# Projecting the first two context tiles side by side, with VectorE taking the first tile's high part

## The reference

```python
def rms_norm(x, w, eps=1e-6):
    return x * rsqrt(mean(x * x, axis=-1)) * w              # per head of 128

xn = layernorm(x)                                            # 256 x 512, own rows
q, k, v = xn @ wq, xn @ wk, xn @ wv                          # 16, 4 and 4 heads of 128
k_ctx, v_ctx = ctx @ wk_ctx, ctx @ wv_ctx                    # ctx 4096 x 512, 4 heads each
q, k, k_ctx = rms_norm(q, q_norm_w), rms_norm(k, k_norm_w), rms_norm(k_ctx, k_norm_w)
q, k = rope(q), rope(k)                                      # own rows only
out = softmax(q @ concat(k_ctx, k).T * scale + mask) @ concat(v_ctx, v)
x = x + out @ wo
```

## Time and profile before

| | us |
|---|---|
| median of three runs | 1070.31 |
| profiled execution | 1069.87 |
| its span | 1067.9 |
| PE busy | 1044.2 |
| DVE busy | 751.1 |
| ACT busy | 551.4 |
| POOL busy | 139.7 |
| mean granted TensorE clock | 0.997 |

### The profile page before, as it was taken

The page is one execution under the profiler, slowest core; times in us unless marked ns, Lnnn a source line. Parts: engine busy times, 40 slices in busy tenths (PEclk is TensorE's granted clock), DMA queues, the critical chain, the costliest instruction groups (busy, mean ns, idle before and its releaser), DMA issues.

```text
span 1067.9 us, 15861 instructions
## 1 busy us (share of the span) xinstructions
PE 1044.2 (98%) x6109; PEld 904.5 (85%) x6109; DVE 751.1 (70%) x1634; ACT 551.4 (52%) x956; POOL 139.7 (13%) x142
## 2 busy tenths in 40 slices
PE   7999999999999999999999999999998799999998
PEld 5888888877888888888888888888776599999997
DVE  5856777649677777777777777777178676776675
ACT  4444443334766556666655666667035354445442
POOL 4644434330000000000000000004121000000000
PEclk9999999999999999999999999999999899999999
DMA  6758676497004220044102340024520195555540
GB/s 231 250 188 290 200 235 197 153 312 274 1 1 169 79 89 2 1 168 129 40 1 90 118 133 1 1 90 160 223 92 1 62 353 191 187 195 180 187 167 21
DMA packets 64155, 145.77 MB, mean 137 GB/s; under 512 B 3889, under 2 KB 42705, under 8 KB 62673
## 3 DMA queue, kind: packets, MB, share of 16 engines
q1 hardware_dynamic: 64080, 144.77, 39.1%
HBM read 108.55 MB, written 36.21 MB: 136 GB/s over the span
## 4 chain that ended last, share of the span: by engine, by line
PE 92%; DVE 5%; ACT 2%; issue 1%; DMA 0%; POOL 0%; POOLq 0%; ACTq 0%
PE bank L435 41%; PE bank L454 16%; PE bank L556 12%; PE bank L533 11%; PE bank L557 6%; PE bank L596 2%; PE bank L464 1%; DVE conv_acc L1033 1%; PE bank L722 1%; PE bank L609 1%; PE bank L489 0%; DVE conv_acc L1030 0%; DMA w_ctx_raw<-in_w_ctx 0%; ACT xc L1397 0%; PE bank L640 0%
## 5 line engine op out<-in xcount | busy, mean ns | idle before, releaser
L969 DVE TENSOR_TENSOR pT<-bank,pT 128x512 fp32r<-128x512 f32 x272 | 184.7, 689 | 112.7 <-ACT pT L1364 112.4
L1364 ACT CAST pT<-bank 128x512 fp32r<-128x512 f32 x272 | 156.2, 593 | 144.3 <-PE bank L533 140.8
L556 PE MATMUL bank<-pT,vN 128*128 128x512 f32 (+1 forms) x544 | 208.7, 408 | 0.0
L435 PE MATMUL bank<-kT,qT_hi 128*128 128x512 f32 (+2 forms) x576 | 188.6, 408 | 2.1 <-DVE scores L913 2.1
L913 DVE TENSOR_SCALAR_CACHE_REDUCE scores<-bank 128x512 f32<-128x512 f32 x256 | 169.3, 682 | 0.1
L533 PE MATMUL bank<-ident,scores 128*128 128x128 f32 x1072 | 161.3, 272 | 0.4 <-DVE pT L969 0.3
L435 PE MATMUL bank<-fT_hi,e_hl 128*128 128x256 f32 x816 | 156.4, 284 | 2.4 <-DVE fT_lo L1142 1.5
L1335 ACT ACTIVATE scores<-scores,neg_max 128x1024 f32<-128x1024 f32 (+2 forms) x128 | 154.0, 1203 | 5.7 <-DVE neg_max L925 5.7
L557 PE MATMUL bank<-pT,vN 128*128 128x256 f32 (+1 forms) x544 | 152.1, 280 | 0.0
L454 PE MATMUL bank<-w_ctx_hi,ctx_hl 128*128 128x512 f32 x512 | 145.7, 397 | 6.4 <-ACT ctx_hl L1244 6.4
L533 PEld LDWEIGHTS bank<-ident,scores 128*128 128x128 f32 x1072 | 127.7, 141 | 12.8 <-DVE pT L969 1.2
(11 more groups left out here) (202 smaller groups left out, 1340.5 us busy)
## 6 DMA issues: line engine op xcount, KB each, us to landing
e_raw<-in_experts SPq DMA_DIRECT2D x51, 768.0 KB, 4.3
k_spill<-k_stage SPq DMA_DIRECT2D x16, 1024.0 KB, 4.5
v_spill<-v_stage SPq DMA_DIRECT2D x16, 1024.0 KB, 8.4
vN<-v_spill SPq DMA_DIRECT2D x16, 1024.0 KB, 5.2
kT<-k_spill SPq DMA_DIRECT2D x15, 1024.0 KB, 5.2
ctx_raw<-in_ctx SPq DMA_DIRECT2D x15, 512.0 KB, 4.4
w_raw<-in_w_qkv SPq DMA_DIRECT2D x6, 1024.0 KB, 5.2
wo_sb<-in_wo SPq DMA_DIRECT2D x4, 1024.0 KB, 8.5
```

The source lines that it names most:

```text
L435: done = e.matmul(dst, lhs(a), rhs(w), start=first and m == 0, stop=last and m == 2)
L556: e.matmul(halves[:, :, q0:L], vN[:, 0, kt, :], ring[:, :, i * L + q0:(i + 1) * L], start=kt == 0, stop=False)
L969: e.tensor_tensor(ring[:, 1, :], bank[tb][:, :], ring[:, 0, :], ALU.subtract).then_inc(p_lo, 1)
L1364: e.copy(ring[:, 0, :], bank[tb][:, :]).then_inc(p_hi, 1)
```

## The change

PE handles tiles 0 and 1 together in `project_first`: for each part of the weights it issues a product for tile 0 and then the same product for tile 1, except in the last part, where all of tile 0 comes before all of tile 1. It counts `ctx_proj` for tile 0 six matmuls before it does for tile 1. The high part of tile 0 is a copy on VectorE with its own semaphore `first_hi`, ahead of the weights' low parts; ScalarE's high parts begin with tile 1, so that `ctx_hi` counts one less. Tile 1 is loaded third.

The own projections begin at tile 3 (`FIRST_OWN`). The turn of the own rows, their split and the first split of the own weights go from tile 1 to tile 2, the tables for the rotation from tiles 1 and 2 to 2 and 3, the second weight load from SP's tile 0 to tile 1. The layernorm is no longer ahead of `after(0)` on VectorE: its first half comes behind `after(0)` and its second behind `after(1)`, with GpSimd's powers behind those of the keys.

```diff
--- before.py
+++ after.py
@@ -32,7 +32,7 @@
 MASKED = -3.0e38
 NW = 6
 NSTEP = NW * TT
-FIRST_OWN = 2
+FIRST_OWN = 3
 NPT = 4
 NEXP = 4
 EXP_STEP = 1024
@@ -362,6 +362,7 @@
         ctx_total = [16 * (NBATCH // NCR)] * NCR + [16] * BT
         out_sent = sem("out_x")
 
+        first_hi = sem("first_hi")
         wc_hi, wc_lo, ctx_hi, ctx_lo, ctx_proj = sem("wc_hi"), sem("wc_lo"), sem("ctx_hi"), sem("ctx_lo"), sem("ctx_proj")
         ksq_done, kssq_done, krs_done, kn_done = sem("ksq"), sem("kssq"), sem("krs"), sem("kn")
         v_hi, v_lo, k_turned, ks_hi, ks_lo, k_tail = sem("v_hi"), sem("v_lo"), sem("k_turned"), sem("ks_hi"), sem("ks_lo"), sem("k_tail")
@@ -441,15 +442,34 @@
                     done = e.transpose(bank[b][:, k * P:(k + 1) * P], src[:, tt, k * P:(k + 1) * P], ident[:, :])
                 done.then_inc(ln_turned, 1)
 
+            def project_first():
+
+                for k in range(KD):
+                    done = [None, None]
+                    for i, n in (((0, 0), (1, 0), (0, 1), (1, 1), (0, 2), (1, 2)) if k < KD - 1 else [(i, n) for i in range(2) for n in range(3)]):
+                        a, w = PRODUCTS[n]
+                        pe.wait_ge((wc_hi, wc_lo)[w], k + 1)
+                        if a == 0:
+                            pe.wait_ge(*((first_hi, 1), (ctx_hi, 1))[i])
+                        else:
+                            pe.wait_ge(ctx_lo, i + 1)
+                        for j, dst in ((0, bank[i]), (1, bank[2 + i])):
+                            done[i] = e.matmul(dst[:, :], ctx_hl[i][:, a, k, :], w_ctx[w][:, k, j, :],
+                                               start=k == 0 and n == 0, stop=k == KD - 1 and n == 2)
+                        if k == KD - 1 and n == 2:
+                            done[i].then_inc(ctx_proj, 1)
+
             def project(i):
                 z = i % 2
-                if i >= 2:
-                    pe.wait_ge(kn_done, i - 1)
-                    pe.wait_ge(v_lo, i - 1)
+                if i == 0:
+                    project_first()
+                if i < 2:
+                    return
+                pe.wait_ge(kn_done, i - 1)
+                pe.wait_ge(v_lo, i - 1)
                 for k in range(KD):
                     for n, (a, w) in enumerate(PRODUCTS):
-                        pe.wait_ge((wc_hi, wc_lo)[w], k + 1)
-                        pe.wait_ge((ctx_hi, ctx_lo)[a], i + 1)
+                        pe.wait_ge(ctx_lo if a else ctx_hi, i + 1 if a else i)
                         for j, dst in ((0, bank[z]), (1, bank[2 + z])):
                             done = e.matmul(dst[:, :], ctx_hl[z][:, a, k, :], w_ctx[w][:, k, j, :],
                                             start=k == 0 and n == 0, stop=k == KD - 1 and n == 2)
@@ -491,7 +511,7 @@
 
             for i in range(NT):
                 project(i)
-                if i == 1:
+                if i == 2:
                     pe.wait_ge(consts, 7)
                     for tt in range(TT):
                         pe.wait_ge(ln_out, tt + 1)
@@ -868,15 +888,13 @@
                 dve.wait_ge(own_rot, 4 * m + 3)
                 e.tensor_tensor(normed[z][:, :], turned[z][:, :], squares[z][:, :], ALU.add).then_inc(own_rot, 1)
 
+            dve.wait_ge(first_in[0], 16)
+            e.tensor_copy(ctx_hl[0][:, 0], ctx_raw[0][:, 0]).then_inc(first_hi, 1)
             for k in range(KD):
                 dve.wait_ge(wc_hi, k + 1)
                 e.tensor_tensor(w_ctx[1][:, k], w_ctx_raw[:, k], w_ctx[0][:, k], ALU.subtract).then_inc(wc_lo, 1)
             for i in range(NT):
-                if i == 0:
-                    dve.wait_ge(x_in, 16)
-                    for tt in range(TT):
-                        layernorm(tt, tt, xn)
-                if i == 1:
+                if i == 2:
                     for tt in range(TT):
                         dve.wait_ge(xnT_hi, tt + 1)
                         e.tensor_tensor(xnT[:, 1, :, tt * P:(tt + 1) * P], bank[6 + tt][:, :].rearrange("p (k t) -> p k t", k=KD),
@@ -884,7 +902,11 @@
                 if i >= 1:
                     rest_of_k(i - 1)
                 after(i)
-                if i == 1:
+                if i == 0:
+                    dve.wait_ge(x_in, 16)
+                if i < TT:
+                    layernorm(i, i, xn)
+                if i == 2:
                     split_w(0)
                 n, half = step_of(i)
                 if half == 1 and n % TT == 0 and n >= 0:
@@ -1299,18 +1321,18 @@
                 act.wait_ge(w_ctx_in[k], 16)
                 e.copy(w_ctx[0][:, k], w_ctx_raw[:, k]).then_inc(wc_hi, 1)
                 if k == 0:
-                    split_ctx(0)
+                    split_ctx(1)
             for i in range(NT):
-                if i + 1 < NT:
+                if 1 < i + 1 < NT:
                     split_ctx(i + 1)
-                if i == 1:
+                if i == 2:
                     for tt in range(TT):
                         act.wait_ge(ln_turned, tt + 1)
                         e.copy(xnT[:, 0, :, tt * P:(tt + 1) * P], bank[6 + tt][:, :].rearrange("p (k t) -> p k t", k=KD)).then_inc(xnT_hi, 1)
                 if i >= 1:
                     main_of_k(i - 1)
                 after(i)
-                if i == 1:
+                if i == 2:
                     split_w(0)
                 n, half = step_of(i)
                 if half == 1 and n % TT == 0 and n >= 0:
@@ -1496,7 +1518,10 @@
 
             def split_ctx(i):
                 b, s, z = i // BT, i % BT, i % 2
-                pool.wait_ge(ctx_hi, i + 1)
+                if i:
+                    pool.wait_ge(ctx_hi, i)
+                else:
+                    pool.wait_ge(first_hi, 1)
                 e.tensor_tensor(ctx_hl[z][:, 1], ctx_raw[b % NCR][:, s], ctx_hl[z][:, 0], ALU.subtract).then_inc(ctx_lo, 1)
 
             def rope_tables(i):
@@ -1512,14 +1537,13 @@
             for i in range(NT):
                 if i + 1 < NT:
                     split_ctx(i + 1)
-                if i == 0:
-                    for tt in range(TT):
-                        inverse_std(tt, tt)
                 z = i % 2
                 pool.wait_ge(kssq_done, 2 * i + 2)
                 e.tensor_tensor(k_rs[z][:, :], k_ssq[z][:, :], power[:, 0:4], ALU.pow).then_inc(krs_done, 1)
-                if 1 <= i < 3:
-                    rope_tables(i - 1)
+                if i < TT:
+                    inverse_std(i, i)
+                if 2 <= i < 4:
+                    rope_tables(i - 2)
                 n, half = step_of(i)
                 if 0 <= n < NSTEP and half == 0 and n // TT != 1:
                     m = own_index(n)
@@ -1619,9 +1643,9 @@
 
             e.dma_start(w_ctx_raw[:, 0], t["w_ctx"][:, 0]).then_inc(w_ctx_in[0], 16)
             e.dma_start(ctx_raw[0][:, 0], t["ctx"][:, 0]).then_inc(first_in[0], 16)
+            e.dma_start(ctx_raw[0][:, 1], t["ctx"][:, 1]).then_inc(first_in[1], 16)
             for k in range(1, KD):
                 e.dma_start(w_ctx_raw[:, k], t["w_ctx"][:, k]).then_inc(w_ctx_in[k], 16)
-            e.dma_start(ctx_raw[0][:, 1], t["ctx"][:, 1]).then_inc(first_in[1], 16)
             e.dma_start(x_sb[:, :, :], t["x"]).then_inc(x_in, 16)
             load_ctx(1)
             load_w(0)
@@ -1636,7 +1660,7 @@
                     load_ctx((i + 1) // BT + NCR)
                 if i >= 1 and (i - 1) % BT == BT - 1:
                     spill((i - 1) // BT)
-                if i == 0:
+                if i == 1:
                     load_w(1)
                 n, half = step_of(i)
                 if half == 1 and n % TT == 0 and n >= 0:
```

## The result

| | before | after |
|---|---|---|
| median of four runs, us | 1070.24 | 1076.38 |
| lowest and highest | 1069.70, 1070.39 | 1074.13, 1077.18 |
| profiled execution, us | 1069.87 | 1077.18 |
| its span | 1067.9 | 1075.1 |
| mean granted TensorE clock | 0.997 | 0.994 |

The changed kernel is slower by a ratio of 1.0053, 95% interval 1.0041 to 1.0065. The forecast was 1076.1. The profiled execution is the slowest of the four, 1.1 above the forecast, which matters for how its rows are read: part of what it shows is not in every run.

What follows compares the result with a forecast made beforehand. PE was taken as the bound, busy 1044.2 of 1067.9 us, with only the start open. The terms -0.2+2.2+1.7+2.3-0.3 give 5.7 (5.75 unrounded), so 1070.31+5.75 = 1076.1 us; range 1073.2 to 1078.4.

Steps and rivals of the forecast that it cites:

- The sum: All terms together, at the first own projection: 5.75 us later than the old one plus a tile.
- The start: PE starts at 5.94, waits 0.5 for tile 1; tiles 0 and 1 end at 19.9 instead of 20.11: -0.2.
- The wait before the turn: Before tile 0's keys are turned, PE waits from 19.9 to 22.05 for their uncovered normalisation chain: +2.2.
- The wait inside tile 2: In tile 2's projection PE waits from 23.4 to 25.1 for GpSimd's low part, queued behind layernorm work: +1.7.
- The wait at the turned rows: Between row transposes PE waits from 30.05 to 32.4 for VectorE's scaled rows, held twice by GpSimd's subtraction: +2.3.
- The first own projection: After the second four transposes, copying only the second half is 0.25 shorter, so it starts at 39.8: -0.3.
- Hidden: SP's loads move with their steps, weight loads keep three tiles of room; a late key load meets the 2.10 wait.
- B: At the turned rows, no collision or VectorE first: only two waits, +3.6, 1073.9 us; chance 0.23.
- C: TensorE's clock falls in one of the waits, costing 1.7 to at most 3.4: 1077.8 to 1079.5 us; chance 0.13.
- a move before 840 us: Sign that the prediction is wrong: the granted clock moves before 840 us.
- D: In the weights' first part the clock rises earlier, saving at most 2.5: 1073.6 or 1071.4 us; chance 0.09.
- E: Tile 0's key chain runs under PE work, the three waits gone: -0.5, 1069.8 us; chance 0.05.

Runs made afterwards that it cites:

- e11: The changed kernel run once more, with nothing altered: 1077.70 us, ratio 1.0063 to the kernel before.
- e8: Changed kernel with layernorm and own projections back in their old places; side by side order, VectorE copy and early tile 1 load kept: 1072.57 us.
- e2: Changed kernel with both halves of the layernorm (VectorE's and GpSimd's) back ahead of tile 0's keys: 1073.11 us.
- e1: Changed kernel with all of tile 0's 24 matmuls before tile 1's instead of side by side: 1074.16 us.
- e4: Changed kernel with GpSimd waiting for VectorE's scaled rows before it subtracts the low parts of tiles 2 and 3: 1075.51 us.
- e5: Changed kernel with SP's second load of own weights behind the first write of keys and values instead of ahead: 1076.20 us.
- e6: Changed kernel with PE's first two waits filled by dummy transposes, 16 before the first turn and 12 inside tile 2: 1075.17 us.
- e7: Kernel before with only the own projections and what belongs to them one tile later: 1070.95 us.
- e9: Kernel before with the split of the first own weights in two halves and begun earlier: 1069.18 us, ratio 0.9987.
- e10: e9 with the first chunk of scores evicted ahead of the last tile's key scaling: 1068.33 us, ratio 0.9981 to the kernel before.

## Why the prediction was right

**The sum.** 5.75 was forecast at the first own projection; the two executions of the changed kernel show 5.05 and 5.68. The medians differ by 6.14 in the prediction's comparison and by 6.98 in the last one (1077.70 against 1070.72). The releasers and the order of the waits were right. That the sum came out so close is in part luck, since its terms missed by up to 0.9 in both directions.

**The start, -0.2.** PE starts at 5.88 (forecast 5.94), since the copy takes 0.43, less than the 0.55 it was bounded by. Both tiles end at 19.75 in after and at about 20.4 in e11, around the forecast 19.9: -0.36 and +0.28 for the term. Two things vary, when tile 1 lands and when the speed rises. In after tile 1 landed at 5.9, the earliest bound, and PE did not wait for it; in e11 it waited 0.68 and in e8 0.91, inside the 0 to 2.0. The speed rose at about 12.0 in after instead of 11.45, and in the other kernels anywhere from 9.5 to 16. The cold matmul was read too long: four from 7.73 take until 9.44 in after, 0.43 each, where I had read 0.465 from the earlier trace rows and taken 0.455. The two from 10.54 that I read it from are no clean pair: the first stands 0.59 ahead of the second, since PE asks for new weights there, and the second lies partly in the faster stretch. In after only the first two matmuls stand further apart than 0.43: from 5.88 to about 12.0 PE gets through 14, where before it got through 10 from 6.37 to 11.47.

**The wait before the turn, +2.2.** 2.09 and 2.09; 2.07 in e2. Right to 0.1. e1 removes it by the order of the tiles, e8 shows 1.20 of it behind eight transposes.

**The wait inside tile 2, +1.7.** 1.27 undisturbed, 0.4 less. Half of that is GpSimd's: its low part ended 2.86 behind tile 0's keys (21.94 to 24.80) where 3.05 was forecast. The other half is PE's: the turn and the four matmuls behind the first wait take 1.58 in e11 (22.64 to 24.22), not 1.35.

**The wait at the turned rows, +2.3.** 1.44 undisturbed, 0.9 too large. The mechanism is shown by e4: GpSimd won both races, the rows read 1.49. Mis-sized was the end of the race: I let the scaled rows begin only when the subtraction ended, +0.55; they end 0.29 behind it, twice, which is 0.5 of the 0.9, since the first race delays the second. The rest is the chain between them, 0.25 shorter than summed, and PE, 0.2 later at its transposes.

**The first own projection, -0.3.** From the second transposes it takes 7.53 in after and in e11 (39.10-31.57, 39.73-32.20) where 7.4 was forecast.

The waits sum to 5.31 in e11 (0.68, 2.09, 1.27, 1.44, less the 0.17 by which its last wait for weights is below before's 0.68), where the prediction had 6.7 for the same four with its 0.5 for tile 1. The missing 1.4 was made up by what the sum had as gains or not at all: the start without its wait brought 0.4 instead of 0.7, with the speed up only at about 12.2; the last term without its wait cost 0.1 instead of bringing 0.3; and PE took 0.7 longer than summed for its work around the waits (the turn and four matmuls, 1.58 for 1.35, is the largest part). That these add up to the same is chance.

**"Hidden" did not hold everywhere.** I moved SP's second weight load past the write of tiles 0 and 1 and said only that the loads keep room. What is behind a moved wait counts too: the write waited with the load, and tile 4 with the write. It is small (0.36 at tile 4, 0.1 at 240 us by e5).

**The rivals.** B (no collision) falls with the 1.49 against 0.55. C (the clock falls in a wait) happened in the profiled execution at 22 us and again at 247, where the prediction had said that a move before 840 us would make it wrong. By that sign it failed in this execution, and held in e11. The fall at 22 cost nothing at the own projection (e6); the one at 247 cost 1.35, near the 1.7 that C took as its lower price, and it came in e7, e8 and e9 too, whose starts are unlike. D and E did not come. In no changed kernel did the speed rise early enough to pay for the waits. The upper end of the range was called the middle of C; the middle of 1077.8 and 1079.5 is 1078.65, not 1078.4, and nothing hangs on it.

**What no run settles.** After's profiled fall explains 1.35 of its own 7.2, not the median's excess. In e11, without a fall, the work behind the scores is reached 6.09 later than in before (250.22 against 244.13) and yet the span has grown by only 5.1 (1073.0 against 1067.9): the unchanged rest of the kernel came out 1.0 shorter in that pair. The runs with low mean clock are longer, but only the profiled execution shows where the clock falls, so how much of the 6 to 7 us at the median is clock is open. The parts as measured are e7 +0.65 and e8 +2.27 against before in the same comparison (together 2.9, where e2, which has both, shows 3.0), and the place of the layernorm, 2.7 between after and e2: 5.6 of 6.1. None of these is sharper than about 1 us.

## What to carry to other kernels

Before work that covered a chain is moved, follow that chain by its rows and write down what PE will ask for at each of its steps: here the layernorm behind the keys and the late end of tile 0 opened some 5 us of waits to win 0.5 at PE's start. Where waits on PE are fed by one chain of other engines, only the chain's length counts; filling PE between them gave nothing here (e6). Split a long step that is late, and pull the eviction that the next product waits for ahead of work that can wait: e9 and e10 are together 2.4 us below the kernel before at the median, of which the rows of the two edits show about 1 (0.4 to 0.5 at the own projection, 0.6 at the scores).
